# Feed-forward stage of a convolution and attention hybrid: fillers, a PSUM bank, the cast to fp8 and the copy of the down product

## What is computed

```python
def _qlinear(x, W, b):
    y = q_acc(jnp.einsum('bsk,nk->bsn', q_mul(x), q_mul(W)))   # q_mul: fp8 (5, 2), q_acc: fp16
    return q_acc(y + q_mul(b))
h = jax.nn.relu(_qlinear(x, W1, b1))      # 24 -> 96
y = _qlinear(h, W2, b2)                   # 96 -> 24
...
t = t + _L2_attn_ref(_ln_t(t), ...)       # the mixer
t = t + _L2_ffn_ref(_ln_t(t), ...)        # layer 0
t = t + _L3_attn_ref(_ln_t(t), ...)
t = t + _L3_ffn_ref(_ln_t(t), ...)        # layer 1
```

## Time and profile before

| | us |
|---|---|
| median of 3 runs | 3226.18 (3224.16 to 3227.25) |
| profiled execution | 3225.27 |
| its span | 3223.6 |
| TensorE busy | 2754.5 (85%) |
| VectorE busy | 1683.6 (52%) |
| ScalarE busy | 1580.7 (49%) |
| GpSimd busy | 365.9 (11%) |

### The profile page before, as it was taken

One profiled execution on the slowest core, in us unless ns is written; L12 is line 12 of the kernel. 1 busy time (PEld: TensorE's weight loads), 2 busy tenths in 40 slices (PEclk: granted clock), 3 DMA queues, 4 the chain that ended last, 5 costly groups with the idle time before them and its releaser, 6 DMA issues.

```text
span 3223.6 us, 109859 instructions
## 1 busy us (share of the span) xinstructions
PE 2754.5 (85%) x49138; PEld 1794.1 (56%) x49138; DVE 1683.6 (52%) x2710; ACT 1580.7 (49%) x2899; POOL 365.9 (11%) x574
## 2 busy tenths in 40 slices
PE   5977889888798887998889988889888998889887
PEld 3537556476464664555735647447465474554754
DVE  5624557355563555535565454744457355573555
ACT  3541555634565335654256442663535635456355
POOL 4620110000100001001010010100110001100011
PEclk8988999999999999999999999999999999999999
DMA  2313000210002100011001100021000210001100
GB/s 82 66 45 75 1 16 6 55 34 2 17 5 54 34 2 17 17 50 26 2 17 36 48 9 2 18 55 35 2 2 19 55 35 1 2 20 35 35 1 17
DMA packets 28433, 84.78 MB, mean 26 GB/s; under 512 B 22002, under 2 KB 23138, under 8 KB 24114
## 3 DMA queue, kind: packets, MB, share of 16 engines
q1 hardware_dynamic: 26690, 72.55, 9.4%
q0 software_dynamic: 1280, 5.21, 0.6%
HBM read 61.70 MB, written 14.84 MB: 24 GB/s over the span
## 4 chain that ended last, share of the span: by engine, by line
PE 67%; ACT 12%; issue 8%; DVE 7%; SPq 3%; DMA 2%; ACTq 0%; DVEq 0%
PE ps L1182 67%; ACT area_ty L904 3%; SPq L513 2%; ACT area_ty L896 1%; DMA area_hz<-f_all 1%; ACT lv L736 1%; DVE area_hz L1031 1%; ACT area_ty L763 1%; ACT area_hz L807 1%; DVE xs L1133 1%; ACT sq L723 1%; DVE area_hz L1048 1%; ACT area_ty L758 1%; DVE area_ty L1156 1%; DVE area_ty L1122 1%
## 5 line engine op out<-in xcount | busy, mean ns | idle before, releaser
L1182 PE MATMUL ps<-area_hz 32*49 32x147 f32 (+3 forms) x7180 | 364.4, 288 | 92.6 <-DVE area_hz L1031 24.1
L872 ACT ACTIVATE area_hz<-ps 121x384 f32<-121x384 f32 (+2 forms) x256 | 129.6, 519 | 584.4 <-PE ps L1182 584.4
L1182 PE MATMUL ps<-area_ty,area_hz 113*64 113x49 f32 (+2 forms) x10240 | 406.6, 255 | 8.5 <-ACT area_ty L786 8.0
L1182 PEld LDWEIGHTS ps<-area_hz 32*49 32x49 f32 (+3 forms) x7180 | 291.0, 151 | 188.0 <-issue 165.0
L1182 PEld LDWEIGHTS ps<-area_ty,area_hz 113*64 113x64 f32 (+2 forms) x10240 | 316.8, 132 | 81.4 <-issue 80.3
L1182 PE MATMUL ps<-area_ty,g_sb 56*112 56x192 f32 (+1 forms) x3712 | 311.6, 321 | 26.0 <-DVE area_ty L1122 19.7
L1182 PEld LDWEIGHTS ps<-area_ty,g_sb 56*112 56x112 f32 x3712 | 293.2, 173 | 44.6 <-issue 43.7
L1182 PE MATMUL ps<-xs,keep_sb 64*64 64x448 f32 (+1 forms) x1184 | 188.5, 543 | 144.4 <-ACT area_ty L763 65.4
L1122 DVE COPY area_ty<-ps 120x896 f32<-120x896 f32 (+1 forms) x192 | 164.8, 858 | 235.0 <-PE ps L1182 235.0
L1182 PE MATMUL ps<-sq,keep_sb 64*64 64x392 f32 (+1 forms) x1248 | 238.9, 556 | 43.1 <-ACT sq L723 24.0
L1031 DVE TENSOR_REDUCE area_hz<-ps 113x12 f32<-113x588 f32 x256 | 194.2, 763 | 138.5 <-PE ps L1182 138.5
(11 more groups left out here) (138 smaller groups left out, 4512.8 us busy)
## 6 DMA issues: line engine op xcount, KB each, us to landing
area_hz<-f_all SPq DMA_DIRECT2D x16, 2541.0 KB
xw<-x_in SPq DMA_DIRECT2D x8, 1568.0 KB, 7.0
y_out<-xs SPq DMA_DIRECT2D x32, 252.0 KB
f_all<-piece POOLq DMA_DIRECT2D x16, 317.6 KB, 3.2
area_hz<-raw_in SPq DMA_DIRECT2D x1, 2894.0 KB, 9.9
g_sb<-g_in SPq DMA_DIRECT2D x6, 355.2 KB
area_ty<-area_hz SPq DMA_DIRECT2D x128, 9.2 KB
g_sb<-g_in SPq DMA_DIRECT2D x2, 710.5 KB
```

Source lines behind the costliest of these rows:

```text
L872: act.activation(dst, src, ACT.Relu if st in (ST_H, ST_F2) else ACT.Copy).then_inc(sc_kept, 1)
L1182: return pe.matmul(o, a, b, start=start, stop=stop)
```

## The change

Four edits of the stage, all in `ffn` and its helpers:

1. Fillers. The two of slot 1 and those at the end of slots 8 and 9 are taken out. Fillers of 320 columns are put in: one in slot 1 ahead of the variance, one in slots 0 and 1 ahead of the centering, and in layer 0 one in slots 9 and 10 at the same place. The last stands ahead of the layer-1 mixer's own fillers.
2. The last side centering of layer 0 goes to bank 1, and no longer waits for `side_logged` of the tile ahead.
3. GpSimd casts each third of `r16` as soon as its L1156 is done; L1156 waits for the same third of the tile ahead to be cast, and each of the three parts of the down product for its own third.
4. The copy of the down product to fp16 goes from ScalarE to VectorE, ahead of L1145.

```diff
+def side_center_bank(which, i):
+    return 1 if (which, i) == (LN_MIX(1), NT - 1) else 3
...
-                    gp.wait_ge(f_relu, (q * 2 * NT + k + 1) * HC)
                     if k >= 2:
                         gp.wait_ge(f_down, q * 2 * NT + k - 1)
-                    gp.sem_inc(passed_gp, 1)
-                    gp.tensor_copy(hq8[:, i % 2, :, :], r16, saturate=False).then_inc(f_hid, 1)
+                    for m in range(HC):
+                        gp.wait_ge(f_relu, (q * 2 * NT + k) * HC + m + 1)
+                        gp.sem_inc(passed_gp, 1)
+                        gp.tensor_copy(hq8[:, i % 2, m, :], r16[:, m, :], saturate=False).then_inc(f_hid, 1)
...
-                    if 0 <= s - 2 < NT:
-                        k = l * NT + s - 2
-                        act.wait_ge(f_down, q * 2 * NT + k + 1)
-                        if s - 2 >= 2:
-                            act.wait_ge(f_bias, q * 2 * NT + k - 1)
-                        act.activation(o16[:, s % 2, :], ps[:, 7, 0:TT], ACT.Copy
-                                       ).then_inc(f_out, 1)
...
+                        ve.wait_ge(f_down, q * 2 * NT + k + 1)
+                        ve.tensor_copy(o16[:, s % 2, :], ps[:, 7, 0:TT]).then_inc(f_out, 1)
...
-                            if m == 0 and k >= 1:
-                                ve.wait_ge(f_hid, q * 2 * NT + k)
+                            if k >= 1:
+                                ve.wait_ge(f_hid, (q * 2 * NT + k - 1) * HC + m + 1)
...
-            def keep_busy(bank, n):
+            def keep_busy(bank, n, w=TT):
                 for _ in range(n):
-                    mm(ps[:, bank, 0:TT], K("center"), keep_sb[:, 0:TT])
+                    mm(ps[:, bank, 0:w], K("center"), keep_sb[:, 0:w])
...
+                    if s == 1:
+                        keep_busy(4, 1, 320)
                     if 0 <= s - 1 < NT:
...
+                    if s <= 1 or l == 0 and s in (NT + 2, NT + 3):
+                        keep_busy(4, 1, 320)
                     if new:
...
-                        if new[1] >= 1:
+                        if new[1] >= 1 and side_center_bank(*new) == 3:
                             pe.wait_ge(side_logged, side_count(q, *new) - 1)
...
-                        pe.wait_ge(f_hid, k + 1)
-                        pe.sem_inc(passed_pe, 1)
                         for m in range(HC):
+                            pe.wait_ge(f_hid, k * HC + m + 1)
+                            pe.sem_inc(passed_pe, 1)
                             ins = mm(ps[:, 7, 0:TT], ffn2[:, l, m, :], hq8[:, i % 2, m, :],
                                      start=m == 0, stop=m == HC - 1)
                         ins.then_inc(f_down, 1)
...
-                        if i == 0:
-                            keep_busy(4, 2)
...
-                    if l == 0 and NT < s < FFN_SLOTS - 1:
-                        keep_busy(4, 1)
```

More of the change, by code:

```diff
@@ L757, in square_side @@
                     act.wait_ge(side_var_made, n - 1)
-                act.activation(side_sq[:, 0:w], ps[:, 3, 0:w], ACT.Square).then_inc(side_squared, 1)
+                act.activation(side_sq[:, 0:w], ps[:, side_center_bank(which, i), 0:w], ACT.Square).then_inc(side_squared, 1)
             def log_side(q, which, i):
@@ L1141, in ffn @@
                         k = l * NT + s - 2
+                        ve.wait_ge(f_down, q * 2 * NT + k + 1)
+                        ve.tensor_copy(o16[:, s % 2, :], ps[:, 7, 0:TT]).then_inc(f_out, 1)
+                    if 0 <= s - 2 < NT:
+                        k = l * NT + s - 2
                         ve.wait_ge(f_out, q * 2 * NT + k + 1)
@@ L1689, in ffn @@
                             pe.wait_ge(x_loaded, q * 16 + 32)
-                        if new[1] >= 1:
+                        if new[1] >= 1 and side_center_bank(*new) == 3:
                             pe.wait_ge(side_logged, side_count(q, *new) - 1)
                         w, x = ln_width(new[0]), xw if l else xs
-                        across = (3, w, K("center"), x[:, w * new[1]:w * new[1] + w])
+                        across = (side_center_bank(*new), w, K("center"), x[:, w * new[1]:w * new[1] + w])
                     if s < NT:
```

## The result

The changed kernel took 3209.95 us (median of 7 runs, 3205.17 to 3220.41), the kernel before 3227.25 on the same chip (7 runs, 3224.16 to 3233.55): a ratio of 0.9942, interval 0.9923 to 0.9961. That is 17 us less, where 37 were forecast. The profiled execution took 3214.43, with a span of 3212.7 (before: 3223.6). It lies 4.5 above its median, so the two profiled executions are 10.8 apart: what is read from their traces adds up to that, not to 17.

What follows compares the result with a forecast made beforehand. TensorE was taken to bound the kernel (L1182 holds 67% of the chain). Gains of 21.8 (fillers), 10.0 (copy), 1 (tail) and 4 (clock) sum to 36.8 us: 3188.5, 3189 as median; own range 3176 to 3212, with rivals 3167 to 3224.

Steps and rivals of the forecast that it cites:

- start fillers, layer 0: Layer-0 stage start: without two fillers ahead of tile 0's up product, the variance starts 1.56 us sooner per run.
- start fillers, layer 1: Layer-1 stage start: without the two fillers the variance starts at 444.60 instead of 445.77, 1.17 us per run.
- clock of the starts: Layer-1 stage starts: new fillers avoid clock drops that cost 10.5 us; 4 taken, ends 10.5 and -6.
- copy off ScalarE: Slots: L763 comes sooner without the copy on ScalarE; 8 x (0.9 + 0.35) = 10.0 us gained.
- thirds in the slots: Slots 2 to 7: cast thirds take 1.68 us instead of 1.31, first ready far earlier, last slightly later; no cost counted.
- tails: Stage ends: fillers out, own bank, thirds; 0.15 us gained in layer 0, 0 in layer 1, sum 1.
- rest and second mixer: Program outside the stage: no term given; only noted that clock drops elsewhere move with every shift.
- they lie in the waits of 0.80, 0.64 and again 0.80: Stage start: the three new 320-wide fillers, 0.57 us each, fit in TensorE's waits and cost nothing; uncovered, 1.7 per run.
- L763 is last by about 0.16: Layer-0 slots with side work: ScalarE's L763 holds the centering; slots 4, 5 and 6 gain 0.5 us together.
- The 0.4 forecast for slot 7: Slot 7, without L1133: moving the copy off ScalarE gains 0.4 us in layer 0, about 0.35 in layer 1.
- Rival (b)'s second form: Slots: a third slips in ahead of the last L1156, L1133 0.45 late in nine slots a quad; 3223; rival's chance 0.15.
- first form: Slots: L1020 runs before the last third, delaying the down product 0.6 or 0.3; 34 us, 3223; rival (b)'s chance 0.15.

Runs made afterwards that it cites:

- e4: The changed kernel with slot 1's first filler ahead of the wait for the side square instead of behind it; 3203.22 us, ratio 0.9926.
- g1: The kernel before with the filler edits alone; cast, copy and banks as before; 3206.05 us, ratio 0.9923.
- f1: The kernel before with only the down product's copy moved from ScalarE to VectorE; 3241.32 us, ratio 1.0027.
- e1: The changed kernel with GpSimd's cast whole again instead of in thirds; 3202.32 us, ratio 0.992.
- g2: f4 without any filler in the feed-forward stage; 3206.57 us, ratio 0.9917.
- f3: The changed kernel with the cast whole for tiles 0 to 5, in thirds for tile 6 alone, and e4's filler order; 3202.61 us, ratio 0.9917.
- g3: f4 with more implied waits left out of the centering and the variance; 3199.04 us, ratio 0.9901.
- f4: f3 with the centering's implied wait for the previous feed-forward sum left out in layer 0's slots 3 to 6; 3195.56 us, ratio 0.9888.
- e2: The changed kernel with the cast in thirds, none starting before all three ReLU thirds are done; 3227.14 us, ratio 0.9994.

## Why the prediction was right in sign and wrong in size

Term by term, in us of the whole program, a minus being a gain:

| term | forecast | measured | from |
|---|---|---|---|
| start fillers, layer 0 | -12.5 | -12.2 | 8 x (1.56 - 0.03), distances of the trace |
| start fillers, layer 1 | -9.4 | -9.4 + 5.9 | 8 x 1.17; 8 x 0.74, e4 |
| clock of the starts | -4 | -10.5 | no cold start of three; g1 |
| copy off ScalarE | -10.0 | 0 | f1 |
| thirds in the slots | 0 | +16 | 8 x (0.99 + 1.04), the four later distances against before |
| tails | -1 | -10.0 and -4.9 | 8 x 1.25 in layer 0, 7 x 0.70 in layer 1; g1 has 0.93 of the 1.25, thirds against e1 0.37 and 0.8 |
| rest and second mixer | 0 | +14 | 12.2 and 2.2; rest column |

- **Start.** Right to 0.03 us per stage in layer 0: the fillers gave what the earlier trace rows said. In layer 1 the step "they lie in the waits of 0.80, 0.64 and again 0.80" failed: I read it off layer 0 and did not look where the code puts the filler against the wait for the side square.
- **Clock.** I took 4 of 10.5; in g1 and the nine other traces with these fillers all starts are warm, and in g2 without them three go cold.
- **Copy.** "L763 is last by about 0.16" failed. The 0.26 in the earlier trace rows against 0.06 in the earlier trace rows was real, its cause was the list of waits of the instruction itself. The earlier trace rows spoke against it from the start: L763 ended at 738.14, 0.19 ahead of L1133, and so was not last. The 0.4 forecast for slot 7 did not come either: the tails of f1 are as before or 0.1 longer.
- **Thirds.** This is the step that cost most: the prediction gave the thirds no cost in the slots, and they cost 16 us. Rival (b)'s second form is what happened, at 0.26 a slot where the rival said 0.45: the first third starts when the third ReLU does, and the ReLU takes 0.68 instead of 0.33. The condition of its first form (L1019 caught by the third cast) does not show in layer 0's slots: L1019 runs 0.92 there. By the rule of the Trainium skill ("SBUF — State Buffer", "Who interferes with whom") that I cited, the ReLU is caught as well; the trace agrees (0.68 against 0.33), while the cast kept 0.56 against a median of 0.56. That the two exclude each other for a whole instruction isn't shown: the ReLU lost 0.35, less than the cast's 0.56 and near the 0.37 of it that grow with the elements, an estimate from the earlier trace rows. I gave that rival 0.15, although the cast's first possible start, T + 1.0 by my own working, was ahead of the last ReLU's end, T + 1.14: the meeting was in my numbers. (It came still sooner, at T + 0.69.)
- **Tails.** I counted 0.2 of the filler's 0.8 at 753.08, and g1 got 0.93 from the tail fillers: they lay on the chain. The cast in thirds gave 0.8 in layer 1 against e1, and 0.37 in layer 0. The own bank shows no difference of its own: g1, without it, has the tail of e1, which has it.
- **Given back.** The rest of the program lost 51 us of clock instead of 41, and took 12 us more. I named that drops elsewhere move, and gave them no term of their own. Why the kernel before has the least of them is open: all 13 other traces lose 51 to 72. f1, whose warm stages hardly differ, loses 57.8, so neither the new fillers nor the thirds are needed for it; that it is the timing of the stages is a guess, and with one trace of the kernel before, so is that its 40.8 is usual for it.

The measured terms of the stages sum to -25.1, the stages' own times to -26.5 (the difference is in the main the tail of the last stage, 1.25, which they leave out), where -36.8 was forecast; the profiled executions are 10.8 apart, the medians 17. The sign had luck in it: the terms that I had too high or at nothing (copy, layer-1 filler, thirds, rest) cost 46 us against the forecast, which alone would have left the profiled execution 9 us slower than the kernel before. That tails and clock gave 20 more than I counted kept the sign, and nothing in the prediction says why they should.

## What to carry to other kernels

Before two engines are set to finer-grained hand-over, ask which instruction of the one then runs beside which of the other, and who waits for that one; here the finer cast won 5 to 9 us in all at the ends of the stages and lost 16 in their slots. Using it for the last tile alone avoids the loss, but keeps only a third of the gain in layer 1 and none in layer 0 (f3). Where an engine follows its releaser by more than elsewhere, look at the instruction's list of waits before another engine is blamed: write the late wait so that nothing stands behind it. Leaving out implied waits helps only where they stand behind the late one; g3 left out one ahead of it and lost 0.04 a slot. A filler belongs ahead of the wait that it is to fill, and an edit of a few us is read stage by stage, since the clock in stretches that it never touched can move the total by as much.

## What the runs showed of the hardware

- The delay between a releaser's end and TensorE's start depends on where the late wait stands in the list: 0.06 us with nothing behind it, 0.10 with one behind and one ahead (0.11 as f4's rows are rounded), 0.15 with one behind and none ahead, 0.26 with three behind. Waits ahead of it cost nothing (0.06 with one, as with none). The Trainium skill ("Perfetto Trace Analysis", "Identifying Dependency Chains") says that further wait conditions may be inserted as instructions of their own. The traces agree: they show them (L1696 and L1699 before, L1709 in g3), 0.051 us each.
- A ReLU of 448 f16 elements takes 0.33 us on VectorE, and 0.68 when a cast of 448 elements on GpSimd starts with it; the cast stays at 0.56. With the same casts begun behind the last ReLU (e2), or the cast whole (e1), no ReLU takes over 0.34.
- Without fillers (g2) three of eight layer-1 stages began at the 1.2 GHz level (mean clock 0.61 over 13 us) after waits of some 0.8 us of TensorE at the mixer's end; with some 0.57 us of filler in each of three waits (f4) none did.
